# A selective scan whose products with B and C are made in pairs of units (128x1024), with two of six B pairs on GpSimd and du on VectorE

## The reference, cut to what matters

```python
dts, Bs, Cs = split(einsum('bkdl,kcd->bkcl', xs, x_proj_weight), [6, 22], axis=2)
delta = softplus(einsum('bkrl,kdr->bkdl', dts, dt_projs_weight) + bias)
h = exp(d_t[..., None] * A) * h + (d_t * u_t)[..., None] * B_t      # over l
y = einsum('bkdn,bkn->bkd', h, C_t)
ys = ys + Ds * xs                      # then the four directions are summed
y = (y - mean) / sqrt(var + eps) * ln_g + ln_b
```

## Time and profile before

| | us |
|---|---|
| median of 3 runs | 5436.18 (5427.06 to 5442.36) |
| span of the profiled execution | 5432.0 |
| PE busy | 4644.7 (86%) |
| DVE busy | 4515.3 (83%) |
| POOL busy | 4129.8 (76%) |
| ACT busy | 2890.6 (53%) |
| DVE busy between 3000 and 4300 us, within the scan | 1290.2 of 1300 |

### The profile page before, as it was taken

The page is one execution under the profiler, slowest core; times in us unless marked ns, Lnnn a source line. Parts: engine busy times, 40 slices in busy tenths (PEclk is TensorE's granted clock), DMA queues, the critical chain, the costliest instruction groups (busy, mean ns, idle before and its releaser), DMA issues. The chain is left out here.

```text
span 5432.0 us, 72922 instructions
## 1 busy us (share of the span) xinstructions
PE 4644.7 (86%) x15210; PEld 2119.9 (39%) x15210; DVE 4515.3 (83%) x4928; ACT 2890.6 (53%) x4502; POOL 4129.8 (76%) x2854
## 2 busy tenths in 40 slices
PE   7998887956999999963978888888888888888887
PEld 2332554623666666642522222222222222222222
DVE  4776445452599999997969999999999999999996
ACT  6885555621111111111357767777777777777776
POOL 2454545532589898987869999999999999999993
PEclk9998999978999999986989999999999999999998
DMA  2000101067677777744057667666776776677773
GB/s 52 1 1 14 56 22 51 27 191 208 130 146 146 143 146 142 149 85 99 0 142 188 185 186 189 184 185 189 187 189 179 188 189 187 181 188 188 187 186 94
DMA packets 385402, 733.35 MB, mean 135 GB/s; under 512 B 77948, under 2 KB 119080, under 8 KB 370920
## 3 DMA queue, kind: packets, MB, share of 16 engines
q1 hardware_dynamic: 385128, 730.30, 54.8%
HBM read 594.31 MB, written 82.32 MB: 125 GB/s over the span
## 5 line engine op out<-in xcount | busy, mean ns | idle before, releaser
L2194 POOL TENSOR_TENSOR l_hc<-l_h,l_c_rep 128x512 f32<-128x512 f32 x1536 | 1927.8, 1273 | 211.3 <-DVE l_h L2248 181.1
L2248 DVE TENSOR_TENSOR_SCAN l_h<-l_p_da,l_h,l_bu 128x512 f32<-128x512 f32 x1120 | 1403.4, 1269 | 5.0 <-ACT l_p_da L2099 2.5
L2099 ACT ACTIVATE l_p_da<-l_p_da,l_a_neg 128x512 f32<-128x512 f32 x1536 | 1008.1, 657 | 729.3 <-PE l_p_da L1954 713.1
L1400 POOL TENSOR_TENSOR l2b_prod<-l2b_v,l2b_attn 128x1568 f32<-128x1568 f32 x276 | 937.3, 3449 | 232.1 <-ACT l2b_attn L1361 116.7
L1954 PE MATMUL l_p_da<-l_stacked,l_pick 96*128 96x512 f32 x1536 | 908.4, 593 | 190.3 <-DVE l_h L2248 180.5
L2233 DVE TENSOR_TENSOR l_bu<-l_du_rep,l_p_b 128x512 f32<-128x512 f32 x1280 | 840.8, 657 | 27.9 <-DMA l_du_rep<-du_scratch 22.2
L1954 PEld LDWEIGHTS l_p_da<-l_stacked,l_pick 96*128 96x128 f32 x1536 | 293.2, 192 | 1161.0 <-DVE l_h L2248 896.8
L1448 DVE TENSOR_REDUCE l2b_osum<-l2b_prod 128x32 f32<-128x1568 f32 x384 | 665.7, 1780 | 63.0 <-POOL l2b_prod L1400 59.3
L1962 PE MATMUL l_p_y<-l_hc,l_y_pick 128*32 128x512 f32 x3072 | 562.9, 626 | 71.8 <-POOL l_hc L2194 71.7
L1353 ACT ACTIVATE l2b_logits<-l2b_conv,l2b_this_b 98x512 f32<-98x512 f32 x96 | 66.2, 689 | 861.5 <-PE l2b_conv L1318 861.5
L1318 PE MATMUL l2b_conv<-l2b_img_high,l2b_w_conv_high 128*98 128x512 f32 x1344 | 356.2, 418 | 32.2 <-DMA l2b_img_low<-qkv_scratch 32.2
(11 more groups left out here) (261 smaller groups left out, 8495.8 us busy)
## 6 DMA issues: line engine op xcount, KB each, us to landing
l_du_rep<-du_scratch SPq DMA_DIRECT2D x1536, 256.0 KB, 3.8
l2b_img_high<-qkv_scratch SPq DMA_DIRECT2D x192, 306.2 KB, 5.7
l2b_img_low<-qkv_scratch SPq DMA_DIRECT2D x192, 306.2 KB, 9.5
l_stacked<-l_parts SPq DMA_DIRECT2D x512, 96.0 KB, 2.7
l2b_v<-v_scratch SPq DMA_DIRECT2D x192, 152.0 KB, 6.5
qkv_scratch<-l2a_strip SPq DMA_DIRECT2D x32, 840.0 KB, 5.2
du_scratch<-l_du SPq DMA_DIRECT2D x128, 192.0 KB, 2.1
l_w_raw<-L_w_sed SPq DMA_DIRECT2D x32, 576.0 KB, 3.7
```

Source lines behind the costliest of these rows:

```text
L1400: return eng.tensor_tensor(dst.rearrange("q x (dy dx) -> q x dy dx", dx=WIN), window, attn_half[:, :, unit % 2].rearrange("q x (dy dx) -> ...
L2099: act.activation(p_da[i % DAS][:], p_da[i % DAS][:], ACT.Exp, scale=a_neg[:, k * G + GRP[i]:k * G + GRP[i] + 1]).then_inc(s_da, 1)
L2194: pool.tensor_tensor(hc[:, (G * par + i) % HCS, :], h[:, i, :], c_rep[:, par, :], ALU.mult).then_inc(s_hc, 1)
L2248: dve.tensor_tensor_scan(h[:, i, way], p_da[i % DAS][:, way], of, state, ALU.mult, ALU.add).then_inc(s_h, 1)
```

## The change

1. **Pairs.** The products with B and with C take two units at once, 128x1024 instead of 128x512, with B or C read twice along a broadcast dimension. The scans stay single. Of the six B pairs GpSimd takes pairs 2 and 5 (one `pool_bu` buffer of a pair), VectorE the other four (two `bu` buffers of a pair). Before, GpSimd had 2 of 12 units.
2. **du on VectorE.** `delta_u` reads delta from PSUM (`p_bc`) and stands behind the scans of pair 1. `low_mm` now waits for it, since it overwrites `p_bc`.
3. **Four decay buffers.** `p_da` holds two pairs. A replica waits for the scan four units back instead of three. In exchange `p_y` is one bank instead of two.
4. **Softplus.** `kept` is gone; log takes 1 + e directly (bias), the constants come from a 97th row, and `delta_sum` of a step is made in the step before it instead of two before. The number of matmuls stays the same.
5. **Order.** TensorE: in a step n, the two halves of `delta_sum(n+1)` behind the replicas of pair 0 and pair 1, `low_mm(n+1)` behind those of pair 3, with two `y_triple` and the `y_whole` of step n-1 between. SyncE: `store_du` before `restack`.

```diff
-    HCS = 8
-    DAS = 3
-    BUS = 3
+    HCP = 4
     RING = 8
-    ON_POOL = (5, 11)
-    BU_AHEAD = 4
+    POOL_PAIRS = (2, 5)
+    DVE_PAIRS = tuple(p for p in range(PAIRS) if p not in POOL_PAIRS)
...
+            def low_mm(m):
+                pe.wait_ge(s_du, m + 1 + DU0)
+                pe.matmul(p_bc[0:C, :], ident, dd[:], start=True, stop=False)
                 pe.matmul(p_bc[0:C, :], minus_r[:], parts[:, 0, :], start=False, stop=True).then_inc(s_lomm, 1)
...
+                replicate(n, k, 0, par)
+                if n1:
+                    delta_rest(n + 1, n + 1)
+                replicate(n, k, 1, par)
+                if n1:
+                    delta_sum(n + 1)
+                if before:
+                    y_triple(n - 1, 2, 1 - par)
+                replicate(n, k, 2, par)
+                if before:
+                    y_triple(n - 1, 3, 1 - par)
+                    y_whole(n - 1, *before)
+                replicate(n, k, 3, par)
+                if n1:
+                    low_mm(n + 1)
+                    b_mm(n + 1, 1 - par, *n1)
+                replicate(n, k, 4, par)
+                if n2:
+                    dt_mm(n + 2, *n2)
+                y_triple(n, 0, par)
+                replicate(n, k, 5, par)
+                if n1:
+                    c_mm(n + 1, *n1, n2)
+                y_triple(n, 1, par)
...
             def step(b, n, k, c, par, n1, n2, before):     # ScalarE
+                c_copy(n, par)
+                decays(n, k, c, 0)
+                log_1e(n + 1)
+                decays(n, k, c, 1)
+                delta_and_high(n + 1, 1 - par)
+                decays(n, k, c, 2)
+                take_y(n - 1, *before)
+                low(n + 1)
+                decays(n, k, c, 3)
+                b_copy(n + 1, 1 - par)
+                ...
+                decays(n, k, c, 4)
+                abs_relu(n + 2, n2[1]); exp_x(n + 2)
+                decays(n, k, c, 5)
+                one_plus(n + 2)
...
             def step(b, n, k, c, par, n1, n2, before):     # GpSimd
+                times_c(n - 1, 5, 1 - par)
+                times_b(n, 2, par)
+                times_c(n, 0, par)
+                times_c(n, 1, par)
+                times_c(n, 2, par)
+                times_b(n, 5, par)
+                times_c(n, 3, par)
+                times_c(n, 4, par)
...
             def step(b, n, k, c, par, n1, n2, before):     # VectorE
+                times_b(n, 1, par)
+                scan(n, k, c, 0, par)
+                scan(n, k, c, 1, par)
+                delta_u(n + 1, *n1)
+                times_b(n, 3, par)
+                scan(n, k, c, 2, par)
+                times_b(n, 4, par)
+                scan(n, k, c, 3, par)
+                scan(n, k, c, 4, par)
+                times_b(n + 1, 0, 1 - par)
+                scan(n, k, c, 5, par)
```

More of the change, by code:

```diff
@@ L1830, in ring_count, with hc_at, end_column @@
             return 16 * (G // 4 * (n - par) // (RING // 4) + (G * par + i) // RING) + 16
-        def vector_bus(i):
-            return sum(j not in ON_POOL for j in range(i))
+        def hc_at(par, p):
+            return 2 * ((PAIRS * par + p) % HCP)
+        def end_column(k):
+            return N - 1 if k < 2 else 0
         def stacked_by(m, par):
@@ L1928, in b_mm @@
                 pe.nop(nofuse=True)
[L1929 to L1944, removed]
+                pe.matmul(p_b[par], w_rep[:, k, 0, :], u_of(b, k, c), start=True, stop=True).then_inc(s_b, 1)
@@ L2151, in _ @@
+                if k == 0 and isinstance(c, int) and c < 2:
+                    turn_x(b, 2 * c + 1)
             for m in range(2):
@@ L2196, in step @@
[L2196 to L2207 removed]
+                for e in range(2):
+                    pool.wait_ge(s_dur[ring_at(par, 2 * p + e)], ring_count(n, par, 2 * p + e))
+                    pool.nop(nofuse=True)
@@ L2250, in step, with delta_u @@
-            def step(b, n, k, c, par, n1, n2, before):
-                for i in range(G):
-                    if i < G - 1 and i + 1 not in ON_POOL:
-                        times_b(n, i + 1, par)
-                    if i == G - 1 and n1:
-                        times_b(n + 1, 0, 1 - par)
-                    scan(n, k, c, i, par)
+            def delta_u(m, b, k, c):
+                dve.wait_ge(s_hi, m + 1 + HI0)
+                dve.wait_ge(s_dus, 16 * m + DUS0)
+                dve.tensor_tensor(du[:], p_bc[0:C, :], u_of(b, k, c), ALU.mult).then_inc(s_du, 1)
@@ new lines, in scan @@
+            def scan(n, k, c, p, par):
+                way, end = slice(None) if k < 2 else slice(None, None, -1), end_column(k)
+                dve.wait_ge(s_hc, PAIRS * (n - 1) + p + 1 + HC0)
+                if p in POOL_PAIRS:
+                    dve.wait_ge(s_pbu, NP * n + POOL_PAIRS.index(p) + 1 + PBU0)
+                    of = pool_bu
+                else:
+                    dve.wait_ge(s_bu, NB * n + DVE_PAIRS.index(p) + 1 + BU0)
+                    of = bu[:, DVE_PAIRS.index(p) % 2]
+                for e in range(2):
+                    i = 2 * p + e
+                    dve.wait_ge(s_da, G * n + i + 1)
+                    state = 0.0 if isinstance(c, int) and c == 0 else h[:, i, end:end + 1]
+                    dve.tensor_tensor_scan(h[:, i, way], p_da[p % 2][:, e, way], of[:, e, way], state,
+                                           ALU.mult, ALU.add).then_inc(s_h, 1)
```

363 lines of the change are left out of this document (157 added, 206 removed).

## The result

The changed kernel takes 5541.29 us (median of 4 runs, 5531.23 to 5551.52), the kernel before 5431.62 us beside it (5423.89 to 5442.36, 4 runs). The ratio is 1.0201, 95% interval 1.0188 to 1.0214: 2% slower, where 1.1% faster was forecast (5375, with a range of 5336 to 5490). The profiled execution has a span of 5549.4 us, against 5432.0.

A forecast was written before the change was run, and what follows sets the result against it. VectorE's own sum bounded the kernel before, 20.08 us a step; after, 19.34 plus a 0.26 average wait for the du replica gives 19.60. Over 128 steps that is -61 us: 5375 us, range 5336 to 5490.

The forecast's parts named there:

- VectorE's sum: VectorE's instructions in one scan step, without waits: 19.34 us after, 0.74 less; -95 us if nothing else binds.
- GpSimd's pair: A two-unit product on GpSimd: pitch taken as 2.38 us, eight pairs 19.0 us a step, below VectorE's 19.34.
- rival 3: GpSimd becomes the bound: a pair costs twice a single, 20.2 us a step, +10, 5446 us; chance 0.12.
- the loop: Low part, restack, du replicas, next step's first pair product, last scans, TensorE's next chain: 19.60 us a step; chance 0.5.
- L: From VectorE's start of `times_b` of pair 1 to low part ready: 8.69 us with contiguous `y_whole`, 9.12 with strided.
- Rival 2: The loop is longer and the kernel slower; with a replica landing of 4.6 us, 20.6 a step, +67, 5503; chance 0.2.
- Rival 4: VectorE's longer products and GpSimd's hold one another up, by one pair a step: 5678 us; chance 0.01.
- From L to the product: From the low part's end through restack and du replicas to the next step's first pair product: 7.20 us.
- a replica's landing: DMA landing time of a replica: 3.0 to 6.0 us, median 4.0; the first step's second one about 3.6.

The follow-up runs named there:

- e2: The changed kernel with SyncE issuing the first two du replicas of the next step ahead of the restack: 5311.67 us, 0.9778 of before.
- e5: The changed kernel with one extra matmul a step that nobody reads, ahead of the replicas of pair 1: 5415.19 us, 0.9973 of before.
- e9: e6 with two matmuls a step that nobody reads, put behind the replicas of pair 2: 5325.25 us, 0.9797 of before.
- e4: The changed kernel with `y_whole` reading contiguously in all steps, so the sum takes wrong positions: 5419.54 us, 0.9971 of before.
- e8: e2 with du back on GpSimd, behind the B product of pair 2: 5401.26 us, 0.9946 of before.
- e6: e2 with `low_mm` also moved ahead of the last triple and `y_whole`, and `take_y` behind pair 3's decays: 5405.11 us, 0.9949 of before.
- e7: The changed kernel with SyncE's store of du behind the restack, as before the change: 5982.74 us, 1.1015 of before.

## Why the prediction was wrong

**Held.** VectorE's sum (forecast 19.34, 19.22 in e2); GpSimd's pair (forecast 2.38 a pitch; a pair lasts 2.37), so rival 3 is out; the place and nature of the loop; L at the full clock, 8.51 and 9.15 against 8.69 and 9.12. Rival 2 had the sign and nearly the time (5503) with the wrong mechanism: it asked for a landing 1.0 us longer. Rival 4 shows nowhere: both engines' products last what they should.

**Failed.** The step is "TensorE's pitches, from the earlier trace rows", taken with the clock of before, "at a granted clock of 0.99", and from it "low part ready at L = 8.69, 9.12". L was 10.69 and 12.20 in the two steps at 4010.87 and 4032.39. The clock was treated as a constant of the kernel, though the change puts TensorE's wait for the last scans right ahead of its part of the loop. By the table, steps at the full clock would take 19.86 in the mean (64 x 19.45 and 62 x 20.28 over 126), and all steps take 21.09: the falls are 1.23 us a step, 157 us in all. e5 bears it out with the loop left alone: 19.93 a step in place of 21.07, by one matmul that nothing reads.

A second term was mis-sized. From L to the product 7.20 us was forecast; where the product waited it was 7.46 (median, 7.18 to 8.76). So the loop at the full clock takes 19.86 and not 19.60, 33 us in all, nearly all of it in the strided steps (20.28, forecast 19.82). Of a replica's landing, 5.2 us in the median over 4000 to 4300 against the 4.0 of the earlier trace rows, the first two replicas of a step paid only this. Together 1.49 a step, times 128 is 191, which with the forecast 5371 makes 5562 against a span of 5549.

**Why it feeds itself.** A fall makes the low part late, so the replica is late, VectorE's product waits, the last scans come late, TensorE's gap before the next chain grows, and the clock falls again. The steps show it: behind a product that waited 0.8 us or more for its replica, 72 of 88 chains met the half level, behind one that waited less, 3 of 38. And falls come in rows: 65 steps with one are followed by another such step and 10 by one without; 41 without are followed by another without. In e5 the waits are there but the gap is filled, and only 5 of 29 waits of 0.8 us or more are followed by a fall. In before no product waited for a DMA, so no fall could come back to TensorE this way: falls are few (20 to 22 steps), and its steps with one take 20.19 us, against 20.05; the 8 with two take about 21, so a fall isn't always free there either. The rule I should have weighed against the sum is in the Trainium skill (TensorE: Matmul & The Clock Gate, "Part 1: The HAM clock gate"): the clock follows how busy the engine has recently been. The windows above agree; that the clock fell behind waits of 1.17 and 0.67 us, after 8.00 us with TensorE busy 7.39, only the trace shows.

**Left open.** The last 14 us between e9 and e2. Why a gap of the same kind is at times followed by no fall and at times by two: 16 of the 88 long waits had none behind them. The share of the loop and of the clock in e4's 122 us. Why GpSimd's pair takes 2.41 us in e8 and 2.37 in the changed kernel.

## What to carry to other kernels

If a change puts TensorE on a loop of dependencies, price its part of the loop at both clock levels, and look at whether the stretch right ahead of it holds a gap that the change lengthens: the clock average of 0.99 before said nothing about it. An engine that issues DMAs strictly in its own order couples transfers that have nothing to do with one another; a load whose data are long there belongs ahead of the transfer that waits, and here this one move was worth 230 us. Where a gap can't be removed, a matmul that nobody reads can be the cheapest repair, as long as it fits in the gap.

## What was unexpected of the hardware

The granted clock went to 0.50 behind 4.60 us in which TensorE was still busy 2.76; no long idle time was needed. Opening the loop at the DMA doesn't by itself make falls cheap: in e6 steps with one take 20.00 and with two 21.22, against 19.18 with none. In e7 the same effect brought a stretch of 2200 us to 0.85 with TensorE busy 1784 of it; the busy share of 81% hides it, since work at the half level takes longer. GpSimd's 128x1024 product costs 2.37 us, 7% less than two of 128x512 at 1.273, although one operand is read twice along a broadcast dimension.
